# A four-layer graph network on one core: the second feed-forward bias is added to x by VectorE ahead of the residual sum, and every engine's order is written anew

## The reference, cut to what matters

```python
h = jnp.maximum(_layernorm(x, axis=-1), 0.0)
x = x + _L0_gnn_ref(h, adj, ...)
# in _L0_gnn_ref, x being h:
x = x + out                                   # masked attention, 8 heads
y = layer_norm(x, gamma2, beta2)
mlp = jax.nn.gelu(y @ W1 + b1, approximate=False) @ W2 + b2
return x + mlp
```

## Time and profile before

| what | value |
| --- | --- |
| median of 3 runs | 4099.08 us (4099.06 to 4100.69) |
| the profiled execution's own time | 4089.18 us |
| its span | 4087.4 us |
| busy: PE, PEld, DVE, ACT, POOL | 96%, 51%, 78%, 52%, 9% of the span |
| granted TensorE clock, mean | 0.99 |
| chain that ended last | PE 88%, DVE 4%, DMA 3%, ACT 2% |
| DMA | 195.29 MB in 212395 packets, q1 busy 15.9% of 16 engines |

### The profile page before, as it was taken

How to read it: one execution, slowest core, us unless ns; L and a number is a source line. 1 busy time by engine, 2 the same in 40 slices (tenths; PEclk the granted TensorE clock), 3 DMA queues, 4 the chain that set the end, 5 groups by cost and what they waited for, 6 DMA issues and landing times.

```text
span 4087.4 us, 80874 instructions
## 1 busy us (share of the span) xinstructions
PE 3930.4 (96%) x33830; PEld 2065.8 (51%) x33892; DVE 3201.5 (78%) x6281; ACT 2121.0 (52%) x3297; POOL 352.2 (9%) x465
## 2 busy tenths in 40 slices
PE   5799999999999999999999999999999999999996
PEld 2345555455555455555455555455555455555553
DVE  6587778887778887778887778887778877778854
ACT  3455555655555654555554455555455554555532
POOL 0001001001000001000101000001000000100000
PEclk9899999999999999999999999999999999999997
DMA  3011211111211111211112111112211111111000
GB/s 109 32 32 58 58 53 37 43 43 58 58 51 39 41 44 58 58 48 42 32 53 58 58 46 44 32 53 58 58 39 48 32 55 58 58 38 42 22 32 32
DMA packets 212395, 195.29 MB, mean 48 GB/s; under 512 B 144448, under 2 KB 179008, under 8 KB 203584
## 3 DMA queue, kind: packets, MB, share of 16 engines
q1 hardware_dynamic: 212032, 190.12, 15.9%
HBM read 138.95 MB, written 17.56 MB: 38 GB/s over the span
## 4 chain that ended last, share of the span: by engine, by line
PE 88%; DVE 4%; DMA 3%; ACT 2%; issue 1%; POOL 1%; SPq 0%; POOLq 0%; DVEq 0%; ACTq 0%
PE M L445 11%; PE M L458 11%; PE O L496 10%; PE S L379 7%; PE S L553 6%; PE O L392 6%; PE M L522 6%; PE O L569 6%; PE O L511 5%; PE M L469 4%; PE M L435 3%; PE M L420 3%; PE O L404 3%; PE M L533 3%; PE M L610 2%; PE O L581 1%
## 5 line engine op out<-in xcount | busy, mean ns | idle before, releaser
L1061 DVE SCALAR_TENSOR_TENSOR PG<-g,tcg,mT 128x512 f32<-128x512 f32 x1024 | 705.7, 738 | 269.8 <-DMA g<-t_rows 233.3
L652 ACT ACTIVATE PP<-S,reach 128x1024 f32<-128x1024 f32 x512 | 544.9, 1112 | 332.4 <-PE S L379 282.0
L940 DVE TENSOR_TENSOR PP<-PP,mT 128x1024 f32<-128x1024 f32 x512 | 603.1, 1213 | 13.6 <-ACT PP L652 12.8
L496 PE MATMUL O<-PG,V 128*32 128x512 f32 x4096 | 525.0, 604 | 21.4 <-DVE PG L1061 21.4
L682 ACT ACTIVATE z<-x,nb,rs 128x256 f32<-128x256 f32 x384 | 202.5, 591 | 585.5 <-DVE nb L931 585.5
L445 PE MATMUL M<-hT,W 128*128 128x512 f32 x1024 | 459.3, 602 | 2.3 <-ACT hT L692 2.0
L458 PE MATMUL M<-W,H 128*128 128x256 f32 x2048 | 459.7, 378 | 0.0
L458 PEld LDWEIGHTS M<-W,H 128*128 128x128 f32 x2048 | 377.3, 189 | 71.7 <-issue 10.6
L771 ACT ACTIVATE PP<-S,sh 128x1024 f32<-128x1024 f32 x256 | 277.1, 1113 | 180.2 <-PE O L569 86.8
L1172 POOL TENSOR_SCALAR ve<-mv 128x4 f32<-128x4 f32 x192 | 87.5, 455 | 3153.6 <-DVE mv L899 2938.2
L949 DVE TENSOR_TENSOR Q<-PP 128x1024 f32<-128x1024 f32 x256 | 301.4, 1218 | 25.0 <-PE O L404 25.0
(11 more groups left out here) (134 smaller groups left out, 5091.8 us busy)
## 6 DMA issues: line engine op xcount, KB each, us to landing
g<-t_rows SPq DMA_DIRECT2D x64, 1024.0 KB, 4.7
adj<-adj_in SPq DMA_DIRECT2D x32, 1024.0 KB, 5.6
x<-x_in SPq DMA_DIRECT2D x32, 512.0 KB, 3.8
z<-t_rows SPq DMA_DIRECT2D x64, 256.0 KB, 3.9
out<-x SPq DMA_DIRECT2D x32, 512.0 KB, 2.9
W<-w_in SPq DMA_DIRECT2D x1, 3072.0 KB, 12.8
mT<-z SPq DMA_TRANSPOSE x128, 2.5
m<-V SPq DMA_TRANSPOSE x128, 2.5
```

The source lines that it names most:

```text
L496: m = e.matmul(k.O[0][r:r + 32, :], s.V[:, jt, 64 * hh + 32 * v:64 * hh + 32 * v + 32], p[:, u, :], start=(jt == 0), stop=(jt == NT - 1))
L652: e.activation(p[:, 2 * pair:2 * pair + 2, :], k.S[:, 2 * pair:2 * pair + 2, :], ACT.Exp, bias=k.reach[:, 7:8], scale=SC0).then_inc(k.e0.s ...
L940: e.tensor_tensor(p[:, 2 * pair:2 * pair + 2, :], p[:, 2 * pair:2 * pair + 2, :], s.mT[:, jt:jt + 1, :].to_broadcast([128, 2, N]), ALU.mul ...
L1061: e.scalar_tensor_tensor(out=p[:, u, :], in0=s.T[hh], scalar=s.tcg[:, 1, hh, jt:jt + 1], in1=s.mT[:, jt, :], op0=ALU.max, op1=ALU.mult).th ...
```

## The change

`b2` moves from the weights that are loaded first to those that are kept, in f32 and on all partitions. A new step `xb` on DVE adds it to x over all four tiles, and `resid0` waits for it. The bias matmul in `w2` goes, the first of the 8 matmuls starts the sum. The tile `b2s` and its preparation in `prep_w` go as well. Besides, steps change places in all lists.

```diff
-KEPT = SMALL + [("W1", 2048), ("W2", 2048), ("Wq", 512), ("Wk", 512), ("Wv", 512), ("Wo", 512)]
+KEPT = SMALL + [("W1", 2048), ("W2", 2048), ("Wq", 512), ("Wk", 512), ("Wv", 512), ("Wo", 512), ("b2", 256)]
 FIRST = [("g1", 256), ("GW1", 512), ("GW2", 512), ("as1", 256), ("ad1", 256), ("as2", 256), ("ad2", 256),
-         ("b2", 256), ("bo", 256)]
+         ("bo", 256)]
...
-        self.wait_ge(k.b_ready, 2)
-        e.matmul(k.M[t % 2][:, 0:256], k.onesb[:, :], k.bias["b2"][:, :], start=True, stop=False)
         for kk in range(8):
             self.wait_ge(*k.gelu.at(b, kk))
             m = e.matmul(k.M[t % 2][:, 0:256], k.H[:, kk, 128 * t:128 * t + 128], w2[:, kk, :],
-                         start=False, stop=(kk == 7))
+                         start=(kk == 0), stop=(kk == 7))
...
-            self.part("b2", k.w("b2"))
...
+    def xb(self, b):
+        e, k, s = self.e, self.k, self.k.of(b)
+        self.wait_ge(k.w_kept, 16)
+        self.wait_ge(*k.z0.at(b, 3))
+        self.mark(e.tensor_tensor(s.x[:, :, :], s.x[:, :, :], k.w("b2")[:, None, :].to_broadcast([128, NT, D]),
+                                  ALU.add), "second bias", 0, b, 0)
...
     def resid0(self, b):
         e, k, s = self.e, self.k, self.k.of(b)
+        self.marked("second bias", 0, b, 0)
         self.wait_ge(*k.add[0].at(b, 3))
...
 def tensor_program(do):
...
         do.wo(b6, 0)
         do.wo(b6, 1)
+        do.qt(b3, 0)
         do.gpv(b5, 2, 3, 1)
         do.gden(b5, 2, 3)
-        do.qt(b3, 0)
...
 def vector_program(do):
...
         do.gvals(b4, 1)
+        do.zb(b3)
         do.wo(b6, 0)
-        do.zb(b3)
+        do.xb(b3)
         do.wo(b6, 1)
...
 def sync_program(do):
...
         do.masks_t(b1, 1)
+        do.rrow(b4)
         do.loada(b0)
-        do.rrow(b4)
```

More of the change, by code:

```diff
@@ L142, in __init__ @@
         self.hi, self.mid = (self.Gf[:, NFIRST + 256 + 128 * i:NFIRST + 384 + 128 * i].bitcast(BF16) for i in range(2))
-        self.bias = {"b2": sb("b2s", [128, D], BF16), "bo": sb("bos", [128, D], BF16)}
+        self.bias = {"bo": sb("bos", [128, D], BF16)}
         self.reach = sb("reach", [128, 8])
@@ L240, in g_value @@
         return self.Gp[b % 2][:, LEAD:].rearrange("p (t h w) -> p t h w", t=NT, w=32)[:, :, :, 0]
-NCONST = 9
+NCONST = 8
 def step(part):
@@ L304, in fin, with xb @@
     def fin(self, b, L, t): pass
+    def xb(self, b): pass
     def resid0(self, b): pass
@@ L604, in wo @@
         self.take(f"M{tp}", k.woa.at(b, tp))
-        self.wait_ge(k.b_ready, 2)
+        self.wait_ge(k.b_ready, 1)
         for t in (2 * tp, 2 * tp + 1):
@@ L998, in resid0 @@
     @step
+    def xb(self, b):
[4 more added lines that the diff above has]
+                                  ALU.add), "second bias", 0, b, 0)
+    @step
     def resid0(self, b):
         e, k, s = self.e, self.k, self.k.of(b)
+        self.marked("second bias", 0, b, 0)
         self.wait_ge(*k.add[0].at(b, 3))
@@ L1281, in tensor_program @@
         do.pv3(b6, 2, 1)
+        do.prep_b(b4)
         do.tt(b4, 0, 0)
@@ L1396, in tensor_program @@
         do.pj(b4, 2, 3)
-        do.prep_b(b3)
 def scalar_program(do):
@@ L1405, in scalar_program @@
         do.ln2(b4, 0)
-        do.pj(b5, 2, 2)
         do.ln2(b4, 1)
@@ L1422, in scalar_program @@
         do.w1(b4, 6)
+        do.sum3(b6)
         do.ln0(b3, 0)
-        do.sum3(b6)
         do.w1(b4, 7)
@@ L1438, in scalar_program @@
         do.pj(b4, 1, 0)
+        do.ln1(b3, 1)
         do.pj(b4, 1, 1)
-        do.ln1(b3, 1)
         do.pj(b4, 1, 2)
@@ L1476, in scalar_program @@
         do.ex0(b3, 5, 1)
+        do.qk(b5, 3)
         do.lnz(b4, 2, 0)
         do.lnz(b4, 2, 1)
-        do.qk(b5, 3)
         do.vp(b5, 0)
@@ L1502, in scalar_program @@
         do.pj(b4, 2, 1)
+        do.pj(b4, 2, 2)
 def vector_program(do):
@@ L1514, in vector_program @@
         do.gvals(b5, 2)
+        do.gw(b5, 2, 0, 0)
         do.bag(b3, 0, 3)
         do.prep_w(b4)
-        do.gw(b5, 2, 0, 0)
         do.resid0(b4)
-        do.masks(b3, 1)
         do.nb(b3, 0)
         do.gw(b5, 2, 0, 1)
-        do.diag(b4)
+        do.masks(b3, 1)
         do.gw(b5, 2, 1, 0)
@@ L1525, in vector_program @@
         do.bst(b3, 1, 1)
+        do.diag(b4)
+        do.bst(b3, 1, 2)
         do.w2(b4, 0)
         do.bst(b4, 3, 0)
-        do.bst(b3, 1, 2)
         do.w2(b4, 1)
+        do.bst(b4, 3, 1)
         do.bst(b3, 1, 3)
[L1531 to L1534, removed]
         do.bag(b3, 1, 0)
-        do.bag(b4, 3, 0)
         do.bag(b3, 1, 1)
@@ L1539, in vector_program @@
         do.bag(b3, 1, 3)
+        do.w2(b4, 2)
+        do.bst(b4, 3, 2)
+        do.gw(b5, 2, 1, 1)
+        do.bag(b4, 3, 0)
         do.bag(b4, 3, 1)
@@ L1574, in vector_program @@
         do.fin(b5, 2, 0)
+        do.b2r(b5, 2, 2)
         do.fin(b5, 2, 1)
         do.bst(b5, 5, 0)
-        do.b2r(b5, 2, 2)
         do.gw(b4, 1, 2, 1)
+        do.fin(b5, 2, 2)
         do.bag(b5, 5, 0)
         do.b2r(b5, 2, 3)
-        do.fin(b5, 2, 2)
+        do.bst(b5, 5, 1)
         do.fin(b5, 2, 3)
-        do.bst(b5, 5, 1)
         do.bst(b5, 5, 2)
@@ L1611, in vector_program @@
         do.pa0(b3, 1, 1)
+        do.bst(b4, 4, 0)
         do.fin(b4, 1, 2)
-        do.bst(b4, 4, 0)
         do.fin(b4, 1, 3)
         do.bst(b4, 4, 1)
+        do.bst(b4, 4, 2)
         do.bag(b4, 4, 0)
-        do.bst(b4, 4, 2)
         do.bst(b4, 4, 3)
@@ L1635, in vector_program @@
         do.sh3(b5, 0)
+        do.pa0(b3, 3, 0)
         do.sh3(b5, 1)
         do.sh3(b5, 2)
-        do.pa0(b3, 3, 0)
         do.pa0(b3, 3, 1)
@@ L1641, in vector_program @@
         do.sc3(b5, 0, 1)
+        do.pa3(b5, 0)
         do.bst(b2, 0, 0)
-        do.pa3(b5, 0)
         do.sc3(b5, 1, 0)
@@ L1647, in vector_program @@
         do.b2r(b3, 0, 1)
-        do.sc3(b5, 1, 1)
         do.fin(b3, 0, 0)
         do.b2r(b3, 0, 2)
+        do.sc3(b5, 1, 1)
         do.fin(b3, 0, 1)
@@ L1671, in vector_program @@
         do.pj(b4, 2, 2)
+        do.sc3(b5, 3, 0)
         do.pj(b4, 2, 3)
-        do.sc3(b5, 3, 0)
         do.gmax(b4, 2)
```

## The result

The changed kernel takes 4144.88 us (median of 5 runs, 4136.24 to 4147.25), the kernel before on the same chip 4099.08 (5 runs, 4091.86 to 4100.81). The ratio is 1.0102, with a 95% interval of 1.0091 to 1.0114: slower by 1%, outside the predicted range. The profiled execution took 4136.74 us with a span of 4134.9, that is 47.5 us more than the span before.

The account below looks back on a forecast made before the run. PE was taken to set the pace, with DVE or a DRAM chain nearly as limiting in places. Terms -13.7 + 35 - 5.3 - 9.5 + 1.4 = +7.9 us, less 2 against the median, gave 4105 us, range 4086 to 4119.

Parts of the forecast that it names:

- The bias matmuls, -13.7 us: Feed-forward, where PE alone decides: 128 bias matmuls of 0.107 us go, gaining 13.7 us.
- `xb` at nothing: DVE around layer 3's projection: the addition fits the gap between the projection's halves, zb the idle time ahead; cost nothing.
- the rival in which DVE has no room: Layer 3's projection: xb ends behind the second half, adding up to 1.22 us an iteration; 4113 us for 0.3; chance 0.08.
- SP's order, +35 us: Layer 3's row: its reads queue behind the adjacency load, so PE starts the projection 1.25 us later in 28 iterations.
- The 5.3 us of late write landings given back: Layer 3's projection: late landings of the row's write cost nothing more while PE waits for the load's packets; 5.3 us gained.
- The late rows of layer 1, 9.5 us given back: Behind the projection: layer 1's row gets about 1.0 us of slack, returning 9.5 of 17.8 us of late rows.
- larger and gives nothing back: Rival: layer 1's row write queues behind load and reads, late rows stay, stall 1.6 us; 4126 us, chance 0.12.
- The small moves at nothing: `qt` ahead of the last `gpv` on PE, small moves on ACT and DVE: taken as 0, at most 3.4 us.
- The start, +1.4 us: First batch: xb waits for the load of W, so scores come 0.5 to 3.3 us later; 1.4 taken.
- The rival in which the reads are not held up: Layer 3's row reads land no later than before, so only the bias matmuls count; 4087 us, chance 0.2.
- The end of "over 3 us" for the stall: Upper end at layer 3's projection: reads start afresh once the adjacency load has landed, landing at 1959.6, stall over 3 us.

Follow-up runs that it names:

- e3_bias_alone: Kernel before with the second bias added on DVE, zb ahead of wo and xb between its halves, no other move: 4069.95 us, ratio 0.9963.
- e8_own_queue: e2_sp_alone with the adjacency load issued by ACT behind rd3(b6), about when the row's write is issued: 4156.00 us, ratio 1.0148.
- e11_own_queue_later: e8_own_queue with ACT issuing the adjacency load one step later, behind pj(b4, 1, 0): 4184.53 us, ratio 1.0189.
- e6_busy_wait: e2_sp_alone with 16 more bias matmuls on PE ahead of its wait for hT, later overwritten: 4135.45 us, ratio 1.0104.
- e13_vp_ahead: Changed kernel with the copy vp(b5, 0) on ACT ahead of lnz(b4, 2, 0) and lnz(b4, 2, 1): 4139.14 us, ratio 1.0073.
- e1_sp_back: Changed kernel with SP's order of before, the adjacency load ahead of the row's write again: 4070.55 us, ratio 0.9962.
- e2_sp_alone: Kernel before with only SP's new order, the adjacency load between the row's write and its reads: 4147.71 us, ratio 1.0145.

## Why the prediction was wrong

The sum forecast +7.9 us against the profiled execution; it was +47.5. By the medians 4105 was forecast and 4144.88 measured.

*The bias matmuls, -13.7 us*, and *`xb` at nothing*: right. The tile pitch is 3.47, and `e3_bias_alone` is 16.5 us faster than before, 12.3 of it (28 x 0.44) from the undisturbed periods. So the rival in which DVE has no room falls as well.

*SP's order, +35 us*: right in mechanism, too small in size; this is the step that failed. The prediction reads: "The adjacency load lands 5.6 us after issue, so at 1955.7. The reads' own packets are worth 0.65 x 3.00 = 1.95 us". The second sentence holds: on average of 28 iterations the reads landed 8.58 us behind the write's issue and adj at 6.63, 1.95 apart. The first does not. Of adj's issue and landing, 0.33 + 5.6 = 5.93 was expected. In 24 iterations adj landed at 6.43 on average, and in four at 7.4 to 8.2. The reads behind it hold it up: on ACT's queue the load took 5.47 us where the reads were issued 4.1 us behind it (`e8_own_queue`), and 6.21 where they were issued 0.9 behind it (`e11_own_queue_later`); in the latter the first third of the reads' packets mixes with its last ones. `rb3` started at 8.67 and PE at 9.96 on average, not at 7.93 and 9.2; the 0.70 by which adj came later than 5.93 is nearly all of it. PE waited 57.5 us where 30 to 40 were forecast; the undisturbed period is 123.7 to 124.1, not 122.8.

*The 5.3 us of late write landings given back*: wrong. The step was "While PE waits for adj's packets, a late landing of the row's write costs nothing more". In those four iterations the write took 2.5 to 2.8 us in place of 1.35; adj, issued behind it, came later as well, and `rb3` started at 9.4 to 9.9 against 8.5 in the others. What holds up the write holds up the load. What that is stays open.

*The late rows of layer 1, 9.5 us given back*: right. DVE's idle time for them fell from 13.7 us to nothing, and PE's waits for `PG` by 5.8, although the row's write now lands 2.0 to 3.9 us after its issue. What this gave back lies between these two numbers. The rival "larger and gives nothing back" had the better time, 4126, and half of the mechanism: the stall was larger, and the write of layer 1's row, issued 6.28 us behind layer 3's as before, landed 1.1 us later on average (after 2.92 us against 1.80). But `rb3` moved by 2.2 us, so the late rows did not stay.

*Not in the sum: the clock.* The wait was priced by its length only. 5 projections took 1.67 us more each, 8.4 us in this execution. `e6_busy_wait` shows that PE's idle time is the cause.

*The small moves at nothing*: nearly right without the swap (0.14 us a period), not clearly so with it. ACT's copy of V stood behind steps that wait for DVE, and with DVE later PE's second `sq3` waited for it, 5.0 us in all. By the ratio of `e13_vp_ahead` this was worth up to 0.3%, by its trace nothing.

*The start, +1.4 us*: the first feed-forward began 4.1 us later in this execution, 1.3 later in `e1_sp_back` and 2.9 in `e3_bias_alone` (at 97.97, 95.23 and 96.83; before 93.91). The forecast's range was 0.5 to 3.3: 4.1 lies above it, the other two in it, and single executions don't settle the size.

Together, against `e1_sp_back`, which differs by the swap alone: 53.4 us more waiting for `hT`, 8.4 of clock, 6.2 of waits for ACT (L751 and L640), less 4.4 of late rows, make 63.6; the 28 periods differ by 60.8. The difference of 2.8 is what these views leave unexplained; part of it may be that the waits for V cost less than their length.

*The rival in which the reads are not held up*: wrong, by all runs with the load in this place. The estimate of 4.4 us for adj beside it uses a fit that the Trainium skill (DMA: Bandwidth & Descriptors, "Anatomy of one DMA") gives for DMAs issued by GpSimd, while these are issued by SP; 5.6 was measured.

The chances failed in one place. The end of "over 3 us" for the stall was named and then left out of the range. That term, repeated 28 times, was the whole risk, and its duration of 5.6 us came from loads with nothing behind them; with the reads behind it, the same load could hardly land earlier, but well later. The chances as added up also give "faster" 0.02 more than their parts, which changes nothing.

## What to carry to other kernels

A transfer that is issued just ahead of an awaited one costs up to its packets' time (here 2.2 us of 2.88), and moving it to another queue does not help; moving it behind the last awaited one does, so for each DMA in a list ask who waits next, not whether it is late itself. A wait of PE of some two microseconds can cost nearly its own length again in clock (1.67 us here, in 5 of 27 iterations of the change and in 10 of `e2_sp_alone`), so a term that repeats in each iteration deserves the wider bound. Undo each move of a mixed change by itself: here one swapped pair of lines hid a gain of 0.4% under a loss of 1.4%.

## What was not expected of the hardware

The landings of DMAs in different queues are as little independent as in one: with 0.28 us of lead, a load of 1 MB on ACT's queue delayed a small write on SP's from 1.35 to 3.8 us on average. And the granted clock fell to the lower level behind idle times of PE of 2.19, 2.40, 2.41, 3.12 and 3.36 us in the changed kernel, but not behind others of 2.86 and 2.94, and not at all where PE was given idle work; the rows don't tell what decides between them.
